# Five plain attentions of a post-norm decoder: hardware loop rewritten as an unrolled three-batch pipeline, with the transposed probabilities as matmul weights

## The reference

```python
B, S, D, H, P = (4, 256, 128, 16, 10)      # run at B=8, S=128
Q = (q @ Wq + bq).reshape(bs, sq, h, dk).transpose(0, 2, 1, 3)
K = (k @ Wk + bk)...;  V = (v @ Wv + bv)...
K = jnp.concatenate([pK, K], axis=2);  V = jnp.concatenate([pV, V], axis=2)
scores = jnp.einsum('bhqd,bhkd->bhqk', Q, K) / np.sqrt(dk)
scores = jnp.where(full_mask == 0, -1000000000.0, scores)
attn = jax.nn.softmax(scores, axis=-1)
out = jnp.einsum('bhqk,bhkd->bhqd', attn, V)
return out.transpose(0, 2, 1, 3).reshape(bs, sq, d) @ Wo + bo
...
x = _layernorm(x + <attention>)
```

## Time and profile before

| | us |
|---|---|
| median of 3 runs | 1614.38 (1609.59 to 1614.58) |
| profiled execution, its time | 1616.38 |
| span of its trace | 1614.6 |
| mean granted TensorE clock | 0.757 of full |

### The profile page before, as it was taken

The page is one execution under the profiler, slowest core; times in us unless marked ns, Lnnn a source line. Parts: engine busy times, 40 slices in busy tenths (PEclk is TensorE's granted clock), DMA queues, the critical chain, the costliest instruction groups (busy, mean ns, idle before and its releaser), DMA issues. The chain is left out here.

```text
span 1614.6 us, 18961 instructions
## 1 busy us (share of the span) xinstructions
PE 1016.0 (63%) x6227; PEld 664.0 (41%) x6227; DVE 1063.7 (66%) x2443; ACT 600.4 (37%) x1133; POOL 125.9 (8%) x279
## 2 busy tenths in 40 slices
PE   5844353545884042469888359996874048868987
PEld 3422232323552032458655126664552035535654
DVE  5768889865653989843357659994664857745543
ACT  3534455532443142431145256540551004423333
POOL 0110001010000000000101200001110010110010
PEclk9975565667887566769879669995886559977678
DMA  4000000001227000010000000000000000000000
GB/s 169 1 0 0 0 0 0 0 0 40 81 81 269 1 1 1 1 46 1 1 1 0 0 0 1 1 0 1 0 0 0 0 1 1 0 0 1 0 1 13
DMA packets 25365, 28.90 MB, mean 18 GB/s; under 512 B 657, under 2 KB 22033, under 8 KB 24274
## 3 DMA queue, kind: packets, MB, share of 16 engines
q1 hardware_dynamic: 25298, 28.06, 5.2%
HBM read 18.62 MB, written 9.44 MB: 17 GB/s over the span
## 5 line engine op out<-in xcount | busy, mean ns | idle before, releaser
L1389 DVE TENSOR_TENSOR_SCAN l2a_hs<-l2a_decay,l2a_b_ps 128x512 f32<-128x512 f32 x64 | 78.0, 1221 | 14.3 <-ACT l2a_decay L1319 6.1
L1244 PEld LDWEIGHTS l2a_b_ps<-l2a_diag,l2a_uT 128*128 128x128 f32 x512 | 64.0, 191 | 39.3 <-issue 38.0
L1775 PE MATMUL l1w_mem_ps<-l1a_rows,l1w_post 128*128 128x64 f32 x16 | 4.3, 363 | 110.7 <-DVE l1a_rows L1915 110.7
L1244 PE MATMUL l2a_b_ps<-l2a_diag,l2a_uT 128*128 128x128 f32 x512 | 69.9, 280 | 2.0 <-DVE l2a_hs L1389 1.7
L1252 PE MATMUL l2a_acc_ps<-l2a_hc,pack 128*128 128x512 f32 x128 | 65.5, 595 | 1.0 <-DVE l2a_hc L1400 1.0
L1888 DVE MATCH_REPLACE8 l1w_minus<-l1w_low,l1w_minus 128x129 f32<-128x129 f32 (+39 forms) x264 | 64.4, 261 | 0.0
L1882 DVE MAX8 l1w_low<-l1w_minus 128x8 f32<-128x129 f32 (+37 forms) x332 | 59.6, 258 | 0.4
L400 PE MATMUL l0x_scores<-pack,l0x_prob 128*128 128x128 f32 x128 | 26.2, 372 | 53.2 <-ACT l0x_prob L535 53.2
L1319 ACT ACTIVATE l2a_decay<-l2a_dt,pack 128x1016 f32<-128x1016 f32 x32 | 36.4, 1141 | 45.4 <-DVE l2a_hs L1389 45.4
L1782 PE MATMUL l1w_at_ps<-l1w_post,l1a_rows 128*128 128x128 f32 x256 | 42.9, 343 | 13.4 <-ACT l1a_rows L1826 13.4
L1803 ACT ACTIVATE l1w_score<-l1w_mix_ps 128x264 f32<-128x264 f32 (+7 forms) x29 | 11.4, 446 | 106.3 <-DVE l1a_rows L1915 92.1
(11 more groups left out here) (601 smaller groups left out, 2908.9 us busy)
## 6 DMA issues: line engine op xcount, KB each, us to landing
scores_dram<-l1p_dots SPq DMA_DIRECT2D x8, 1056.0 KB, 5.9
l1a_rows<-scores_dram SPq DMA_DIRECT2D x8, 1056.0 KB, 12.1
pack<-in_pack SPq DMA_DIRECT2D x1, 697.5 KB, 9.7
pack<-in_pack SPq DMA_DIRECT2D x2, 321.5 KB, 7.3
pack<-in_pack SPq DMA_DIRECT2D x1, 612.0 KB, 11.6
pack<-in_pack SPq DMA_DIRECT2D x1, 576.0 KB, 10.6
pack<-in_pack SPq DMA_DIRECT2D x1, 514.0 KB, 8.3
x_tok<-in_x SPq DMA_DIRECT2D x1, 512.0 KB, 4.0
```

Source lines behind the costliest of these rows:

```text
L1244: mm = nc.tensor.matmul(bx_ps(n)[:, j * S:(j + 1) * S], uT[:, c, b, :], diag[:, s % 2, b, :], start=True, stop=True)
L1389: nc.vector.tensor_tensor_scan(hs[:, n % 2, :], decay[:, k % 2, batches, :].rearrange("p b t -> p (b t)"), bx_ps(n), 0.0, ALU.mult, ALU.ad ...
```

## The change

The old function is kept as `distance_attention` and used for l0x alone. A new `attention` serves the five plain ones. What it does otherwise:

- No hardware loop: the iterations `now` = -1 to 9 are unrolled in Python. q, km, v, prob and probT are there twice.
- All scores of a batch, two halves, are made at once: four masks, then four row groups, when both subtractions of the batch before are done.
- Probabilities are turned four heads at a time into a bank of their own (`turn_ps`), and ScalarE empties it after each four (512 columns).
- In `weigh` the turned probabilities of a head are the weights (128 x 128) and nine value columns move; the result is token-major. `transpose_sums` and `copy_sums` are gone.
- q and k are projected two batches further ahead, v one batch; the LayerNorm of a batch runs an iteration later. v is projected straight from the context or `xT`, without `vsrc`.
- In l3x one prefix matmul of 160 columns takes the place of two, VectorE copies its result out first, the prefix is weighed with 256 moving columns, and the value bias comes in at `copy_out` (and is subtracted from the prefix values first), so that the row matmul is gone.

```diff
-def attention(nc, cm, name, kv="x", bias=False, mask=None, project=True, rope=False,
+def attention(nc, cm, name, kv="x", bias=False, mask=None, project=True, rope=False, prefix=False, src="x"):
...
+        qk_bank, sums_bank, row_bank, turn_bank = (sc.ps(n, [128, 512]) for n in ("qk_ps", "sums_ps", "row_ps", "turn_ps"))
+        scores = sc.ps("scores", [128, 2, HALF, S])
...
+                def score(b):
+                    pe.wait_ge(qk_set, b + 1)
+                    after(pe, diff_set, 2 * b)
...
+                        for g in range(HH):
+                            nc.tensor.matmul(bank(g), cm.ident_bf[:], bcast_mid(bias_mask, HH), start=True, stop=False)
+                    for g in range(HH):
+                        rows = slice(32 * g, 32 * g + 32)
+                        mm = nc.tensor.matmul(bank(g), q[b % 2][rows, :], km[b % 2][rows, :, :],
+                                              start=bias_mask is None, stop=True)
...
+                def transpose_probs(b, half, part):
+                    pe.wait_ge(prob_set, 2 * b + half + 1)
+                    after(pe, turn_copied, turn(b, half, part))
+                    for n in range(HH):
+                        mm = nc.tensor.transpose(turn_ps[:, n, :], prob[b % 2][:, half, HH * part + n, :], cm.ident)
...
+                def weigh(b, half):
+                    if half == 0:
+                        pe.wait_ge(v_set, b + 1)
+                        after(pe, o_set, b)
+                    pe.wait_ge(turn_copied, turn(b, half, 1) + 1)
...
+                    for h in range(HALF):
+                        mm = nc.tensor.matmul(sums_q[:, HALF * half + h, 0:DH + 1], probT[b % 2][:, half, h, :],
+                                              v[b % 2][:, HALF * half + h, 0:DH + 1], start=not prefix, stop=True,
...
+                for now in range(-1, B + 2):
+                    if inside(now + 1):
+                        score(now + 1)
...
+                        score_prefix(now + 1)
+                    if inside(now):
+                        transpose_probs(now, 0, 1)
+                    if inside(now - 2):
+                        transpose_norm(now - 2)
+                    if inside(now):
+                        transpose_prefix(now)
+                        transpose_probs(now, 1, 0)
+                    if inside(now + 1):
+                        project_v(now + 1)
+                    if inside(now + 3):
+                        project_qk(now + 3)
+                    if inside(now):
+                        transpose_probs(now, 1, 1)
+                    if inside(now - 1):
+                        transpose_out(now - 1)
+                    if inside(now):
+                        weigh(now, 0)
+                    if inside(now + 1):
+                        transpose_probs(now + 1, 0, 0)
+                    if inside(now - 1):
+                        project_out(now - 1)
+                    if inside(now):
+                        weigh(now, 1)
...
+                for now in range(-1, B + 2):
+                    if inside(now - 2):
+                        statistics(now - 2)
+                    if inside(now + 2):
+                        copy_qk(now + 2)
+                    if inside(now - 2):
+                        ln.dve_scale(dve, nc, cm, now - 2)
+                    if inside(now + 1):
+                        prefix_maximum(now + 1)
+                        maximum(now + 1, 0)
+                    if inside(now - 1):
+                        divide(now - 1)
+                    if inside(now + 1):
+                        maximum(now + 1, 1)
+                        prefix_difference(now + 1)
```

More of the change, by code:

```diff
@@ L123 @@
 }
-ROWS = [("l0f_b2", 128), ("l2a_out_b", 128), ("l1f_ln", 256), ("ones", 128),
-        ("l3x_bv", 128)]
+ROWS = [("l0f_b2", 128), ("l2a_out_b", 128), ("l1f_ln", 256), ("ones", 128)]
 PRE = 10
@@ L253, in attention, with distance_attention @@
+def distance_attention(nc, cm, name, kv="x", bias=False, mask=None, project=True, rope=False,
               prefix=False, distance=False, src="x"):
@@ L2156, in program @@
             if layer == 1:
-                attention(nc, cm, "l0x", kv="ctx", bias=True, mask="ic1", distance=True)
+                distance_attention(nc, cm, "l0x", kv="ctx", bias=True, mask="ic1", distance=True)
             if layer == 2:
@@ L2219, in plain @@
             c[f"{name}_{key}"] = np.asarray(I[f"{full}_{n}"])[:, None]
[L2220 to L2223, removed]
+        c[f"{name}_bv"] = np.asarray(I[f"{full}_{bv}"])[:, None]
         c[f"{name}_bo"] = np.broadcast_to(np.asarray(I[f"{full}_{bo}"])[None, :], (128, D))
@@ L2239, in layout @@
         c[f"l3x_pv{half}"] = a
+        a = np.zeros((128, 32), f)
+        a[0:HALF * PRE, 0:DH] = np.repeat(np.asarray(I["L3_xattn_bv"]).reshape(2, HALF, DH)[half], PRE, axis=0)
+        c[f"l3x_bv{half}"] = a
     layout_more(I, c, r)
```

254 lines of the change are left out of this document (added), and 3 rows, old and new, of the table COLS.

## The result

The changed kernel takes **1679.85 us** (median of 4 runs, 1676.13 to 1693.29) against 1614.48 before: ratio 1.0435, 95% interval 1.040 to 1.047, so 4.4% slower where 0.9% faster was forecast. The range, up to 1635, does not hold it.

A forecast was written before the change was run, and what follows sets the result against it. Neither TensorE nor VectorE is full; in an l1x batch both are close to a chain through two halves. Intervals -38.2, fill and drain +6.5, low clock +16 give -15.7 against 1616.4: 1601, less 2 for the median, rounded 1600 us; range 1574 to 1635.

The forecast's parts named there:

- Prices at the full clock: Half of `weigh`, 16 records of 0.11 us, 1.75 us; four row groups of scores 1.06 us; l1x period 9.5 us.
- The ring: Per batch: scores, first half's maximum and subtraction, division, output transpose, both `weigh` halves, projection; sum 9.7, taken as 9.5 us.
- mishap: Sign of being wrong: full-clock period above 10 us, for example four transposes waiting for the copy of their shared bank.
- The seven intervals: Between first and last of a stage's eight batches: l0a -1.9, l1x +0.3, l2x -5.9, l3a -8.2, l3x -22.5; together -38.2 us.
- Fill: Stage ends: first scores in one piece +0.5, later LayerNorm some +0.8; +1.3 us a stage, +6.5 in all.
- The low clock: At 1.2 GHz a batch takes about 6.3 us more; half a cold batch more per stage, 3.2 us, +16 in all.
- The clock rival: Weight loads in `weigh` and idle TensorE keep the clock low; one more cold batch per stage, 1632 us; chance 0.26.
- the cheap `weigh`: `weigh` under 0.11 us a record, overlapping its loads; VectorE ring of 7.8 us, another -1.5 a batch, 1545 us; chance 0.05.
- Gains by stage: Sign of being right: largest gain in l3x, some 20 us, and none in l0a and l1x.

## Why the prediction was wrong

- **Prices at the full clock: right.** Periods in the run with 64 columns, at the full clock throughout its steady batches, are 9.2, 9.6, 8.7, 9.7, 11.7 us for l0a, l1x, l2x, l3a, l3x; forecast 9.2, 9.5, 8.6, 9.8, 11.8. A half of `weigh` is 16 records in 1.70 us, 106 ns each. The Trainium skill, "TensorE: Matmul & The Clock Gate", section "LDWEIGHTS", gives 107 ns for 128 columns. The trace agrees with that, and not with the 25 ns of its section "Back-to-back issue gap".
- **The ring: right number, partly another way.** I named the division (L582) as TensorE's largest wait. In the steady batch it waits for L451 twice, 1.4 us in 15, the copy out of the one bank of four turned heads, and not for the division at all. I had named that bank only as a mishap.
- **The seven intervals: -38.2 forecast.** In the run with 128 columns, from first to last division: 314.3 us against 367.4 before, -53.1 (rows below: that run, then the kernel before). The last two intervals of l1x take 5.7 and 7.1 us where I had a full period and 7.5.

```profile
L579 DVE RECIPROCAL l0a_rz<-l0a_sums_ps x8: 245/247/258, 43.2 to 101.7; 128x16 f32<-128x16 f32 x8
L579 DVE RECIPROCAL l1x_rz<-l1x_sums_ps x8: 245/248/251, 827.1 to 888.4; 128x16 f32<-128x16 f32 x8
L579 DVE RECIPROCAL l2x_rz<-l2x_sums_ps x8: 246/248/252, 1143.7 to 1200.6; 128x16 f32<-128x16 f32 x8
L579 DVE RECIPROCAL l3a_rz<-l3a_sums_ps x8: 245/246/249, 1345.9 to 1407.7; 128x16 f32<-128x16 f32 x8
L579 DVE RECIPROCAL l3x_rz<-l3x_sums_ps x8: 247/247/258, 1448.7 to 1524.6; 128x16 f32<-128x16 f32 x8
...
L749 DVE RECIPROCAL l0a_rz<-l0a_bankB x8: 246/247/258, 35.8 to 99.3; 128x16 f32<-128x16 f32 x8
...
L749 DVE RECIPROCAL l1x_rz<-l1x_bankB x8: 245/246/258, 825.9 to 889.7; 128x16 f32<-128x16 f32 x8
L749 DVE RECIPROCAL l2x_rz<-l2x_bankB x8: 245/258/258, 1143.1 to 1207.8; 128x16 f32<-128x16 f32 x8
L749 DVE RECIPROCAL l3a_rz<-l3a_bankB x8: 248/251/257, 1347.5 to 1420.2; 128x16 f32<-128x16 f32 x8
L749 DVE RECIPROCAL l3x_rz<-l3x_bankB x8: 257/258/259, 1460.6 to 1563.3; 128x16 f32<-128x16 f32 x8
```

- **Fill: +6.5 forecast, +20 measured** in the same run (first division after the stage's start, against before: 7.3, 2.6, 2.2, 6.9, 0.7 us). The division of the first batch comes an iteration later; I had counted only the scores in one piece and the late LayerNorm. The two errors cancel by luck: -33 for -32.
- **The low clock, +16: the step that failed.** "I charge half a cold batch more per stage" should have been 97 to 108 us, what the runs with 128 and 64 columns win back. The price of a cold batch was near (6.3 for about 7.0), their number was not: by the clocks of the windows the five stages are at the low level for 348 us, and for 73 with 128 columns moving. The 275 between are some 17 batches of 16.5 us, by this estimate, where I charged 2.5. I had read the low clock as a matter of a stage's start, because in l1x nearly all of it lay there, and a new inner loop as neutral to it. The price of `weigh` was worked out in time alone: 16 records of 0.11 us. That TensorE's work in those 1.7 us is of another kind than the 128 moving columns of before was in front of me (2 x 0.64 us of dense work replaced by 3.5 us of loads), and I drew only the +2.2 us from it. I held l0a's 0.99 against it, "with the same steps", which was false: its `weigh` is the step that changes.
- **The rivals.** The clock rival (0.26, 1632 us) had the sign, the mechanism and half the reason: it blamed the loads and the idle stretch. The idle stretch does not exist (4.00 of 4.00 us busy at the fall). It charged one cold batch more per stage than my forecast; l1x at 0.68 is at the low level for 64% of 120 us, 77 us against 29 before, which is three batches more. Its sign, transposes of 0.2 us or more behind the first two batches, came (1.11 us for four at 879.32), and mean clocks below in l1x, l2x and l3a, not in l3x. The transposes themselves are as many in the run with 128 columns, where l0a has 1.00. The Trainium skill, "TensorE: Matmul & The Clock Gate", Part 4, says that the full clock does not engage for transposes; mixed with matmuls, as here, the trace disagrees. The sum for the cheap `weigh` is 1541 by its own terms, not 1545.
- **Gains by stage.** l3x was to gain 22.5 us in its intervals and l0a and l1x to stay as they were; l3x gained 12 over the stage and the two lost 25 and 24.

With more columns moving, the change comes to -27 us (128) and -39 (64), around the -32 of the forecast without the clock's term. So the total of the other terms was near, in part because two of them erred against each other; the clock's term was too small by some 80 to 90 us and outweighed the rest.

Left open: where between 9 and 64 columns the loss ends in each stage. At 32 l0a stays at 0.78, with steady batches of up to 12.8 us, while l1x has 0.85 and holds a steady 9.55.

## What to carry to other kernels

When the smaller operand is made the moving one, the matmul count may stay, but TensorE spends its time loading weights, and the granted clock can fall in the midst of that work: price such a change at both clock levels, and see whether the steady loop can hold the upper one. If two changes come in one, measure them apart; here a gain of 86 us lay hidden under a loss of 156. Padding the moving side with zeros up to 32 columns, which did not lengthen a steady batch of l1x at the full clock (9.55 us for 9.54), was worth 68 us. With 64 it was 108, but that run wrote heads over each other; a correct one of that width was not run. Moving the wide operand, as the old `weigh` does, was worth more than either, 156.

## What the runs showed of the hardware

- The granted clock fell from 2.4 to 1.2 GHz in a stretch with TensorE busy for 4.00 of 4.00 us; stages with 128 x 128 float32 weights and nine moving columns had a mean of 0.67 to 0.76, the same records with 128 columns 0.90 to 1.00.
- Bfloat16 filler of 0.86 us a batch hardly moved the mean clock (0.739 for 0.729), though it held 1.00 in the steady batches of three stages. With 3.5 us it was 0.782, and with float32 filler of the same time the same.
- A float32 matmul with 128 x 128 weights stands as two records, in a row of them 106 ns each with nine moving columns, 109 with 64 and 112 with 128, at the full clock.
- Four row groups of scores run in 1.07 us, the time of two, at the full clock too.
